# Gathers without waits: x for the eight output pieces in buffers of its own, all eight adds on VectorE, and a new order of the expert stage's helpers

## The reference, cut to what matters

```
x  = L0_attn_x                                   # (32, 256, 128) f32
xn = layernorm(x)
# state space layer on xn
u  = xn @ W_x.T + b_x ; g = sigmoid(xn @ W_g.T + b_g)
h  = depthwise conv of width 3 over the sequence of u, + conv_b
u  = u * g + h * (1 - g)
dt = clip(softplus(xn @ W_dt.T + b_dt).mean over all tokens, 0.001, 2)
A_d = exp(-softplus(A_raw) * dt) ; B_d = (A_d - 1) / (A + 1e-6) * B_ssm
y  = linear recurrence over the 256 steps with A_d, B_d, C_ssm
attn = layernorm(xn + y @ W_out.T + b_out) * ln_g + ln_b
# experts on xn: each token goes to experts h and h + 1 (mod 8)
h  = int(xn[0] + xn[1]) mod 8
ffn = 0.5 * sum over the two experts of (relu(xn @ W1 + b1) @ W2 + b2)
out = x + attn + ffn
```

## Time and profile before

| | |
|---|---|
| time, median of 3 runs | 607.81 us (606.57 to 609.21) |
| the profiled execution | 606.78 us, its span 605.0 us |
| busy: PE, PEld, DVE, ACT, POOL | 453.4, 378.7, 397.7, 317.8, 240.0 us |
| mean granted TensorE clock | 0.885 of full speed |
| HBM traffic | 28.12 MB read, 24.25 MB written |

### The profile page before, as it was taken

How to read it: one execution, slowest core, us unless ns; L and a number is a source line. 1 busy time by engine, 2 the same in 40 slices (tenths; PEclk the granted TensorE clock), 3 DMA queues, 4 the chain that set the end, 5 groups by cost and what they waited for, 6 DMA issues and landing times. The chain is left out here.

```text
span 605.0 us, 11873 instructions
## 1 busy us (share of the span) xinstructions
PE 453.4 (75%) x3387; PEld 378.7 (63%) x3387; DVE 397.7 (66%) x665; ACT 317.8 (53%) x898; POOL 240.0 (40%) x273
## 2 busy tenths in 40 slices
PE   1173303239998898999999999999874297989991
PEld 1152202128887898999999998999831143437880
DVE  6893000026674999999999999998120043767697
ACT  2773102028998676767755666665621043433774
POOL 3767777700000223233253456432267604451320
PEclk9998756559999999999999999999985577979997
DMA  9992112101412111221131234312271103417544
GB/s 247 307 361 69 52 52 69 52 27 53 126 30 67 33 37 35 44 43 35 43 81 37 44 92 119 84 36 47 40 187 52 48 2 93 109 40 183 154 121 139
DMA packets 111415, 52.77 MB, mean 87 GB/s; under 512 B 48880, under 2 KB 106392, under 8 KB 111384
## 3 DMA queue, kind: packets, MB, share of 16 engines
q1 hardware_dynamic: 106328, 43.48, 27.2%
q0 software_dynamic: 4096, 8.40, 4.6%
q10 hardware_dynamic: 960, 0.52, 0.3%
HBM read 28.12 MB, written 24.25 MB: 87 GB/s over the span
## 5 line engine op out<-in xcount | busy, mean ns | idle before, releaser
L1439 PE MATMUL PS<-AR 128*128 128x128 f32 x1184 | 138.4, 275 | 1.5 <-ACT AR L769 1.5
L1439 PEld LDWEIGHTS PS<-AR 128*128 128x128 f32 x1184 | 135.2, 192 | 2.1 <-ACT AR L769 2.1
L769 ACT ACTIVATE AR<-PS,VC 128x256 f32<-128x256 f32 x296 | 111.8, 489 | 7.6 <-PE PS L1427 6.6
L1377 PE MATMUL PS<-RR 128*128 128x512 f32 x96 | 44.3, 461 | 65.1 <-ACT RC L689 38.9
L1425 PE MATMUL PS<-XT,RR 128*128 128x256 f32 x296 | 86.0, 291 | 7.0 <-POOL XT L582 5.8
L1426 PE MATMUL PS<-XT,RR 128*128 128x256 f32 x296 | 82.6, 279 | 0.0
L1427 PE MATMUL PS<-XT,RR 128*128 128x256 f32 x296 | 82.5, 279 | 0.0
L608 POOL TENSOR_TENSOR AR<-AR,b2p 128x256 f32 x37 | 37.1, 1003 | 96.5 <-ACT AR L782 96.5
L576 POOL DMA_INDIRECT sorted_tokens<-RA,posi x64 | 61.6, 962 | 23.2 <-issue 22.3
L582 POOL TENSOR_TENSOR XT<-XTF,XT 128x256 fp32r<-128x256 f32 x35 | 32.5, 930 | 89.3 <-ACT XT L746 89.2
L1377 PEld LDWEIGHTS PS<-RR 128*128 128x128 f32 x96 | 20.2, 210 | 74.5 <-ACT RC L689 41.3
(11 more groups left out here) (231 smaller groups left out, 940.6 us busy)
## 6 DMA issues: line engine op xcount, KB each, us to landing
sorted_tokens<-AR SPq DMA_DIRECT2D x10, 512.0 KB, 6.2
XSIN<-sorted_tokens SPq DMA_DIRECT2D x160, 32.0 KB, 1.8
sorted_outputs<-AR SPq DMA_DIRECT2D x37, 128.0 KB, 1.9
RA<-in_L_attn_x_dram SPq DMA_DIRECT2D x8, 512.0 KB, 8.1
normalised_tokens<-RA SPq DMA_DIRECT2D x16, 256.0 KB
RB<-normalised_tokens SPq DMA_DIRECT2D x8, 512.0 KB, 6.1
AR<-in_L_ffn_W_dram SPq DMA_DIRECT2D x15, 256.0 KB, 3.3
out_dram<-RB SPq DMA_DIRECT2D x7, 512.0 KB, 3.2
```

The costliest lines, as they stand in the source:

```text
L769: nc.scalar.activation(HID[n][:, k, :], ps[2 * n + k // 2][:, (k % 2) * FT:(k % 2 + 1) * FT], ACT.Relu, bias=B1C[:, e, k:k + 1]).then_inc( ...
L1377: T.matmul(bank, PW[:, 0, n, :], xh[s], start=True, stop=False)
L1439: ins = T.matmul(ps[5 + h][:, 0:D], HID[n][:, k, h * P:(h + 1) * P], W2S[slot][:, k, :], start=(n == 0 and k == 0), stop=(n == 1 and k == ...
```

## The change: what it does

Memory for x. `XB[0..3]` moves to the upper half of `RC[:, 1, :]` and `XB[4..7]` to the lower half of `RB[:, 0, :]` (the intra matrices, free when the recurrence is done). No `XB` overlaps a `GA` any more, so GpSimd's 64 gathers have no wait between them. Pieces 4 to 7 of the first half of y now wait for `add_x(0..3)`, whose x they overwrite. VectorE does all eight `add_x`: four in the recurrence (duos 5, 7, 10, 13; before three, in duos 6, 10, 13), and four among the output pieces. SP loads x 4 to 7 behind all loads of the normalised tokens, with no waits for single output groups.

Expert stage. GpSimd's low part of tile i + 2 stands behind the bias of tile i, and so ahead of the start of the next group. VectorE starts the gate before the first low part, does the small dt arithmetic behind the gate pieces, and has `ahead(j)` in place of `due`. ScalarE's last `gate_input` of the projection stands behind the split of the second expert weight.

```diff
-        NPL, NPR = 4, 4
-        PLAIN = list(range(NPL)) + list(range(NB8 - NPR, NB8))
-        XB = {n: GA[NAR + n] for n in range(NPL)}
-        XB.update({NB8 - NPR + m: batch(RC[:, 1, :], m) for m in range(NPR)})
+        XB = [batch(RC[:, 1, :], NB8 - NAR + n) for n in range(NAR)] + [batch(RB[:, 0, :], n) for n in range(NB8 - NAR)]
...
-            for n in range(NPL):
+            for n in range(NAR):
                 load_x(n)
             sp.wait_ge(s_yps, PPB)
             sp.wait_ge(s_xnd, 16 * NCH)
             for n in range(NAR):
                 load_xn(n)
-            for n in range(NAR, NB8 - NPR):
-                load_x(n)
             sp.wait_ge(s_yps, NPAIR)
             for n in range(NAR, NB8):
                 load_xn(n)
-            for m in range(NPR):
-                sp.wait_ge(s_po, 2 * m + 2)
-                load_x(NB8 - NPR + m)
+            for n in range(NAR, NB8):
+                load_x(n)
...
+                if 1 <= g < E - 1:
+                    k = g + 2
+                    pool.wait_ge(s_wph, k - 2)
+                    nc.gpsimd.tensor_tensor(W1l[k % 3], ...).then_inc(s_wps, 1)
...
                 with pool.Fori(bounds[g], bounds[g + 1]) as i:
-                    with pool.If(i >= NLOW - 1):
-                        low_part(i + 1)
                     pool.wait_ge(s_ysb, i + 2)
                     nc.gpsimd.tensor_tensor(tile_of(YSB, i), ...).then_inc(s_yad, 1)
+                    with pool.If(i >= NLOW - 2):
+                        with pool.If(i < bounds[E] - 1):
+                            low_part(i + 2)
...
             for n in range(NB8):
-                if n >= NAR:
-                    pool.wait_ge(s_xb, n - NAR + 1)
                 for t in range(TB8):
                     nc.gpsimd.indirect_dma_start(out=GA[n][:, t, :], ...).then_inc(s_gat[n], 16)
-            n = NB8 - 1
-            pool.wait_ge(s_gat[n], 16 * TB8)
-            pool.wait_ge(s_xg[n], 16)
-            pool.wait_ge(s_xb, n)
-            nc.gpsimd.tensor_tensor(GA[n], GA[n], XB[n], ALU.add).then_inc(s_xb, 1)
...
-            gate_input(NCH - 1)
+            act.wait_ge(s_pr[2][HB - 1], NCH)
             high_weights(1)
             softplus(NCH - 1, [1])
+            gate_input(NCH - 1)
...
+            def ahead(j):
+                return (10 * j + 67) // 21
...
-                    due = 4 * (hb * NGATE + n)
-                    tiles_to(4 + 21 * (due - 2) // 60 if due else 3)
+                    third = 3 * (hb * NGATE + n)
+                    tiles_to(ahead(third + 1))
...
+                if hb == 0 and n >= NB8 - NAR:
+                    dve.wait_ge(s_xb, n - (NB8 - NAR) + 1)
...
+            XQ = (DPB - 3, DPB - 1, DPB + 2, DPB + 5)
...
-                if q in (DPB - 2, DPB + 2, DPB + 5):
-                    add_x((q - DPB + 2) // 3)
+                if q in XQ:
+                    add_x(XQ.index(q))
...
-            add_x(3)
             y_piece(1, 4)
-            add_x(4)
...
             add_base(2)
-            add_x(5)
+            add_x(4)
...
             add_base(3)
-            add_x(6)
+            add_x(5)
...
             scale_gain(11)
+            add_x(6)
...
             add_base(6)
+            add_x(7)
```

More of the change, by code:

```diff
@@ L484, in load_x @@
             def load_x(n):
-                sp.dma_start(XB[n] if n in PLAIN else GA[n], x_v[:, n * TB8:(n + 1) * TB8, :]).then_inc(s_xg[n], 16)
+                sp.dma_start(XB[n], x_v[:, n * TB8:(n + 1) * TB8, :]).then_inc(s_xg[n], 16)
             def load_xn(n):
@@ L586, in _ @@
             for g in range(E):
+                if 1 <= g < E - 1:
+                    k = g + 2
+                    pool.wait_ge(s_wph, k - 2)
+                    nc.gpsimd.tensor_tensor(W1l[k % 3], W1RAW[raw_slot(k)], W1h[k % 3].bitcast(F32), ALU.subtract
+                                            ).then_inc(s_wps, 1)
                 pool.wait_ge(s_w2[g % 3], 32 * (g // 3 + 1))
@@ L1039, in _ @@
             bounds = expert_bounds(dve)
-            low_tile(1)
             for hb in range(HB):
-                dve.wait_ge(s_min[hb], NCH)
-                dve.wait_ge(s_ln[hb], NCH)
                 dve.wait_ge(s_ue[hb], NCH)
[L1046 to L1057, removed]
-                link(V.tensor_scalar(aval[:, hb, :], Aneg[:, hb, :], dtv[:, hb, 0:1], None, ALU.mult))
+            dve.wait_ge(s_ws, 2)
+            def ahead(j):
+                return (10 * j + 67) // 21
             def split_weights(k):
@@ L1073, in _ @@
                                                 ALU.mult, ALU.add))
+                    if hb == 0 and n == 0:
+                        low_tile(1)
+                        tiles_to(4)
                     link(V.scalar_tensor_tensor(t3[:, :, 0:L - 1], u3[:, :, 1:L], cwn[:, hb, 2:3], t3[:, :, 0:L - 1],
                                                 ALU.mult, ALU.add))
-                    due = 4 * (hb * NGATE + n)
-                    tiles_to(4 + 21 * (due - 2) // 60 if due else 3)
+                    third = 3 * (hb * NGATE + n)
                     if hb == 0 and n == 0:
                         split_weights(2)
-                        low_tile(2)
+                    tiles_to(ahead(third + 1))
                     dve.wait_ge(s_sig, hb * NGATE + n + 1)
                     link(V.scalar_tensor_tensor(TG, z, 1.0, TG, ALU.subtract, ALU.mult))
+                    if hb == 0 and n == 0:
+                        low_tile(2)
                     link(V.tensor_tensor(z, u, TG, ALU.add))
-                    tiles_to(4 + 21 * (due - 1) // 60 if due else 3)
+                    tiles_to(ahead(third + 2) if third else 5)
                     if hb == 0 and n == 0:
@@ L1092, in _ @@
                                      z.rearrange("p (c i) -> p c i", i=Q)))
-                    tiles_to(4 + 21 * due // 60)
+                    tiles_to(ahead(third + 3))
+            for hb in range(HB):
+                dve.wait_ge(s_min[hb], NCH)
+                dve.wait_ge(s_ln[hb], NCH)
+            dve.wait_ge(s_sumr, 1)
+            V.tensor_reduce(dtv[:, :, 0], acc1[:, :, :], AX_X, ALU.add)
+            link(V.tensor_reduce(dtv[:, :, 1], acc2[:, :, :], AX_X, ALU.add))
+            link(V.tensor_tensor(dtv[:, :, 1], bdtm[:, :], dtv[:, :, 1], ALU.subtract))
+            link(V.tensor_tensor(dtv[:, :, 0], dtv[:, :, 0], dtv[:, :, 1], ALU.add))
+            link(V.tensor_scalar(dtv[:, :, 0], dtv[:, :, 0], 1.0 / NTOK, DT_MIN, ALU.mult, ALU.max))
+            link(V.tensor_scalar(dtv[:, :, 0], dtv[:, :, 0], DT_MAX, None, ALU.min))
+            dve.wait_ge(s_asq, 2)
+            link(V.tensor_tensor(Aneg[:, :, :], sv[:, :, :], sv2[:, :, :], ALU.add))
+            link(V.tensor_scalar(Aneg[:, :, :], Aneg[:, :, :], -1.0, None, ALU.mult))
+            for hb in range(HB):
+                link(V.tensor_scalar(aval[:, hb, :], Aneg[:, hb, :], dtv[:, hb, 0:1], None, ALU.mult))
             dve.wait_ge(s_jv, 2)
@@ L1103, in _ @@
             ins.then_inc(s_earg, 1)
-            tiles_to(26)
+            tiles_to(27)
             for n in range(3 * NTOK // 2 // CH):
@@ L1108, in _ @@
                 if n in (11, 23):
-                    tiles_to(27 + n // 12)
+                    tiles_to(28 + n // 12)
             V.memset(KP.rearrange("p b j -> p (b j)"), 0.0)
@@ L1130, in _ @@
             link(V.tensor_reduce(half[:, :], half4[:, :, :], AX_X, ALU.add))
-            tiles_to(29)
+            tiles_to(30)
             dve.wait_ge(s_eexp, 1)
@@ L1151, in _ @@
             TT = TB[:, 0:HB * Q * Q].rearrange("p (b g i) -> p b g i", b=HB, i=Q)
-            tiles_to(30)
+            tiles_to(31)
             for j in range(Q):
@@ L1155, in _ @@
             link(ins)
-            tiles_to(31)
+            tiles_to(32)
             link(V.transpose(TB[:, 0:HB * Q * Q].rearrange("p (b g i) -> p b i g", b=HB, i=Q), TO))
@@ L1195, in _ @@
             link(ins)
-            tiles_to(36)
             RT = TB.rearrange("p (r a i) -> p a r i", a=2, i=Q + 1)
@@ L1207, in _ @@
                 if ab == 0:
-                    tiles_to(37)
+                    tiles_to(36)
             link(ins)
@@ L1277, in add_base @@
                 dve.wait_ge(s_fp, scaled(2 * n + 1)[1])
-                if n in PLAIN:
-                    dve.wait_ge(s_xb, PLAIN.index(n) + 1)
-                else:
-                    dve.wait_ge(s_gat[n], 16 * TB8)
+                dve.wait_ge(s_xb, n + 1)
                 V.tensor_tensor(VV[n], VV[n], GA[n], ALU.add).then_inc(s_fo, 1)
@@ L1324, in _ @@
                     dve.wait_ge(s_fp, len(VG))
-                    dve.wait_ge(s_xb, NPL + NPR)
+                    dve.wait_ge(s_xb, NB8)
                 else:
```

5 lines of the change are left out of this document (removed).

## The result

| | time, median (lowest to highest) | profiled execution: time, span, mean granted clock |
|---|---|---|
| before | 607.19 us (606.28 to 609.21, 4 runs) | 606.78, 605.0, 0.88 |
| changed | 626.45 us (625.49 to 627.76, 4 runs) | 626.06, 624.3, 0.86 |

The ratio is 1.0288, with the interval 1.0242 to 1.0334: the change costs 19 us. Busy time by stage in the changed kernel, for the same stages as the earlier trace rows: expert stage, recurrence until TensorE runs short, the starved stretch, the rest of the recurrence, output stage.

The account below looks back on a forecast made before the run. TensorE was taken to bound the expert stage and recurrence, starved of instructions while gathers are issued. 606.8 - 5.5 (expert stage) + 21.1 (recurrence) + 0.3 (output stage) = 622.7, predicted as 623 us, range 607 to 629.

Parts of the forecast that it names:

- expert stage: Expert stage: fewer TensorE waits for GpSimd's low part (-5.8) and 0.3 charged give -5.5 us, bounds -7 and 0.
- recurrence: Recurrence: one unbroken run of 64 gathers keeps TensorE short of instructions longer, its end at 565.1 against 544.0, +21.1 us.
- output stage: Output stage: adds in VectorE's closed stretch +2.4, GpSimd's add and a slow VectorE instruction gone -2.1; +0.3 us together.
- One run of 64, with its starved stretch: Sign in the recurrence: 64 gathers 1.25 us apart, about 80 us; TensorE gaps from some 7 us in, 45 to 70 matmuls.
- 31 + 24 = 55: Starved stretch of the recurrence: 31 matmuls as before, plus 24 taken for 40.1 more starved microseconds, between 14 and 35.
- back at speed 4.2 us after the start of the last gather: Recurrence: last gather starts at 520.4 and TensorE recovers 4.2 us later, at 524.6, as after the first 32 before.
- 35.8 + 3.7 + 1.0 = 40.5: Recurrence after the starved stretch: 480 matmuls left take 35.8 us, the restart 3.7, one exposed add 1.0.
- The first rival: Recurrence: starvation does not go on at that rate; each further 8 gathers cost 6.1 us, time 608.7; chance 0.12.
- The second rival: Recurrence: starvation belongs to the first burst, with x loads issued then, not to the gathers; time 584.3; chance 0.07.
- under 1: Sign in the expert stage: TensorE's wait for GpSimd's low part falls under 1 us in total, from 5.8 us.
- the 0.3 charged: Expert stage start: ScalarE's new order has the second weight 0.6 us earlier and the relus 0.6 later; 0.3 us charged.
- the last batch of gathers ... cost TensorE nothing: Output projection, kernel before: the last 8 gathers beside it were free, since TensorE needs fewer instructions there; no size given.

Follow-up runs that it names:

- rows of 128 bytes: The changed kernel with each gather fetching 128 rows of 128 bytes in place of 512, the number of gathers unchanged: 629.15 us, one execution.
- the waits back: The changed kernel with gathers 4 to 7 waiting again for add_x(n - 4): 614.13 us against 610.54 for the kernel before, ratio 1.0074.
- the expert stage alone: The kernel before with only the change's expert-stage edits, its memory and gathers as they were: 609.0 us against 610.54, ratio 0.9953.
- the paced kernel: The changed kernel, gather batches 0 to 3 spread over duos 0 to 9, 4 to 7 behind the last duo: 596.01 us (chip A), 478.17 us (chip B).
- chip A: The chip on which the kernel before takes 607 to 611 us; the result's chip is not recorded but is counted with it.
- SP's loads: The changed kernel with its 64 gathers replaced by 64 plain loads of the same size issued by SP, in stored order: 541.82 us, one execution.
- chip B: One of two other chips on which the kernel before takes 473.5 us; the changed kernel itself was not run there.

## Why the prediction was right, step by step

The time is 626.45 where 623.0 was predicted, slower as forecast and inside 607 to 629. The mechanism, that gathers without pauses keep TensorE short, was right on the chip that it was read from. That what TensorE is short of is instructions, and that a store of them bridges the first microseconds, was the prediction's reading of "issue"; no run shows either. The sum's terms, on the profiled execution:

| term | forecast | measured | from |
|---|---|---|---|
| expert stage | -5.5 | -4.3 | 438.64 to 434.33 |
| recurrence | +21.1 | +28.2 | 105.4 to 133.6 |
| output stage | +0.3 | -4.6 | 61.0 to 56.4 |
| sum | +15.9 | +19.3 | |

*One run of 64, with its starved stretch.* Right: 78.7 us long, TensorE short from 5.8 us after its first, 53 matmuls where 31 + 24 = 55 were forecast. The term of the recurrence was mis-sized in one step, "back at speed 4.2 us after the start of the last gather". That was true of the run of 32; after 64 it took 11.3 us. The longer tail is no accident: with 64 gathers in one run it was 11.3, 10.3 and 10.6 us in three executions (the changed kernel, the same again, and with rows of 128 bytes; recurrence 133.6, 133.3 and 134.2), and behind a run of 32 it was 4.2 us in the kernel before, 6.5 with the waits back, 6.4 with the expert stage alone and 4.8 in the paced kernel's projection. The gap of 9.88 us is something else: it was in two of the three, once from 509.72 across the last gather (516.01) and once over before it, and the third has the same tail without it. The 7.1 us between 4.2 and 11.3 are the whole difference between 21.1 and 28.2. From there on the 40.6 us to the end of the recurrence are what was forecast (35.8 + 3.7 + 1.0 = 40.5): 35.2 for 473 matmuls, 1.85 of adds exposed, and 3.5 that are left for the restart.

*The first rival, and what a run costs.* On chip A the recurrence takes 49.7 us without gathers, so what they cost can be read off by the length of a run. Four runs of 8 (paced) cost 72.4 - 49.7 = 22.7, or 5.7 each; the kernel before (32, 8, 8, 8) costs 55.7, which leaves 38.6 for the 32; with the waits back (32, 16, 8, 8) it is 69.2, which leaves 19.2 for the 16; the 64 cost 83.9. Per gather that is 0.7, 1.2, 1.2 and 1.3 us, and the last three are about the 1.25 us that a gather takes to issue. So in a long run each gather costs about all of its time, and only in a short one do the first few microseconds, in which TensorE goes on, bridge a good part. This is the reading that the prediction took, and it is why the first rival's price of 6.1 us for each further 8 was too low. The subtraction rests on single profiled executions, and gaps such as the 7.79 us one move it by that much. It also takes the paced kernel's last two runs of 8 as apart, with a pause of 1.49 us between them. Taken as one run of 16, the same totals give 3.1 us for a run of 8, 16.6 for 16 and 46.5 for 32. Either way a run of 8 costs less than the 10 us that it lasts, and the prices of 16 and 32 are rough.

*The second rival* (the first burst and not the gathers) fell with SP's loads: the loads of x were still there and nothing starved. On chip B neither the burst nor the gathers starve anything. The Trainium skill, "Runtime: NRT & Kernel Launch", section "Instruction fetch mechanics", calls the cost of crossing from one block of instructions to the next mostly hidden. Chip B agrees with it (no matmul waits for "issue" in 110.9 us with 64 gathers). The prediction said that the rows of the hole don't agree with it, and that is where it read them wrongly: the time isn't lost at such a crossing. In the DMA view of the changed kernel the queue that carries instructions has one packet between 440 and 470, just as the hole begins (the line below), and none from 470 to 530:

```profile
q8 instruction: 1, 0.02, 0.2%
```

With SP's loads the same queue has four packets between 440 and 470, and nothing starves. So on chip A TensorE's 84 us go by while next to no instruction block is fetched, and the rule says nothing of them. To take the rows against "gathers cannot starve straight-line code" was right for the chip that the rows came from; nothing in one trace could say that it held for this chip only.

*The expert stage.* -4.3 for -5.5, for the most part by the mechanism named. The waits for GpSimd's low part fell from 5.8 us in seven to 2.4 in three, where "under 1" was forecast. With ScalarE's new order TensorE waits 1.82 us for ScalarE at 192.36, where it waited 0.67 before (at 192.51), so the 0.3 charged was too low; but it starts no later there. With these edits alone the stage ended 5.4 us earlier.

*The output stage.* Here the step that failed is "the last batch of gathers ... cost TensorE nothing". Of TensorE's busy time that was nearly so (46.5 us before, 45.9 after), but ScalarE was starved beside it. In the kernel before, its squares of the group whose matmuls end at 564.98 stand behind an instruction that ends at 565.36, and begin at 568.55; the releaser that the row names is a group later:

```profile
563.17 2.19 ACT L813 ACTIVATE RB<-PS,fs 128x128 f32<-128x128 f32 x8
568.55 0.28 ACT L821 ACTIVATE RB<-PS 128x128 f32<-128x128 f32 x1 [3.19 <-PE PS L1511]
```

The same pair in the changed kernel has no pause:

```profile
585.37 2.19 ACT L801 ACTIVATE RB<-PS,fs 128x128 f32<-128x128 f32 x8
587.37 0.36 ACT L809 ACTIVATE RB<-PS 128x128 f32<-128x128 f32 x1
```

VectorE's next scale arithmetic (L1252, changed L1251) comes 26.3 us after the stage's start before (570.30) and 21.3 after (589.20): 3.2 us are this pause, and 1.7 are in TensorE's first two groups, which take 6.5 us before and 4.8 after. From there VectorE's closed stretch is 32.0 and 32.3 us: its two adds more and the slow instruction less cancel, as forecast. Eight executions with no DMA of GpSimd beside the projection (five on chip A) have 56.3 to 57.6 us for the stage, the two with the last batch and GpSimd's add beside it 61.0 and 61.1. ScalarE's pause is the gathers' doing by that comparison and not by an experiment on them alone. That a run of 32 in the same place costs 33 us in the paced kernel on chip A (89.2 for 56.4) shows that the stage was never safe.

*The two errors have opposite signs*, and the time is better predicted than its parts: 7.1 us too little in the recurrence, 4.9 us too much in the output stage.

## What to carry to other kernels

Idle time that the profile puts down to "issue", beside a long series of indirect DMAs of GpSimd, can be a cost of those DMAs: break the series into short runs with pauses, or move it, before taking a wait away because it looks idle. Such a wait can be a pacer; price its removal by how long the series gets. And time such a change on more than one chip: the paced kernel is 2% faster than the kernel before on one and 1% slower on another, and both chips run the same program.

## What the runs showed of the hardware that I had not expected

- The same program takes 607 to 611 us (medians) on one chip, on two occasions (26 executions beside the experiments), and 473.5 us on two others (14): the first takes 28% longer. Next to 64 indirect DMAs, 1.25 us apart, TensorE's straight-line code runs at one matmul in 2.80 us on the first and undisturbed on the others. Whether it is the chip or a state that it was in, and what sets them apart, no trace shows; nor was it shown what TensorE is short of on chip A.
- On chip A the starvation depends neither on the bytes (134.2 us at a quarter of them, 133.6 at all) nor on the traffic (166 GB/s of loads by SP: none). It goes on for 10 to 11 us behind the start of the last of 64 gathers, but 4.2 to 6.5 us behind that of the last of 32.
- ScalarE has such a pause too (3.19 us before 568.55 in the kernel before, its input ready), and a run of 32 starves the output projection, which I had thought too thin to starve.
